# A fused transformer-and-scan kernel: the scan running on between sequences, list-scheduled engine orders, and elementwise steps on other engines

## What is computed

```
q, k, v = relu(x @ W.T + b)
attn = softmax(q @ k.T * scale);  y = relu((attn @ v) @ Wo.T + bo)
scores = sqrt(softplus(x @ gate.T)); top 2 of 8 experts by scores + gate_b
h = silu(x @ w1.T) * (x @ w3.T), times the token's weight;  out += h @ w2.T
z, x, B, C, dt = x @ W_in.T;  delta = softplus(dt @ W_dt.T + 2*b_dt)
u = silu(conv4(x) + conv_b)
state = exp(delta * A) * state + delta * u * B     # over 512 tokens, 512 channels x 16 states
y = (sum over states of state * C + u * D) * silu(z);  out = y @ W_out.T
h = relu(x @ W1.T)**2;  out = (h * rsqrt(mean(h**2))) @ W2.T
```

## Time and profile before

| | |
|---|---|
| median of three runs | 2094.04 us |
| profiled execution | 2099.33 us, of which the span is 2097.5 |
| TensorE busy | 1651.5 us (79%) |
| VectorE busy | 1770.0 us (84%) |
| ScalarE busy | 1035.9 us (49%) |
| GpSimd busy | 913.8 us (44%) |
| DMA | 157.95 MB, 75 GB/s over the span |
| granted TensorE clock, mean | 0.90 of full speed |

### The profile page before, as it was taken

The page is one execution under the profiler, slowest core; times in us unless marked ns, Lnnn a source line. Parts: engine busy times, 40 slices in busy tenths (PEclk is TensorE's granted clock), DMA queues, the critical chain, the costliest instruction groups (busy, mean ns, idle before and its releaser), DMA issues. The chain is left out here.

```text
span 2097.5 us, 22567 instructions
## 1 busy us (share of the span) xinstructions
PE 1651.5 (79%) x5875; PEld 725.3 (35%) x5948; DVE 1770.0 (84%) x3142; ACT 1035.9 (49%) x1745; POOL 913.8 (44%) x676
## 2 busy tenths in 40 slices
PE   3375577778996889868997799878997899779856
PEld 1122123232452335322452335332452335234324
DVE  6577899989879998979989998999989987987830
ACT  3247444825555454735556355734547344734312
POOL 0101534454437434554346434464346544665510
PEclk9977699979997999979997899979997899999978
DMA  4100222222222222222231222222222223223300
GB/s 108 46 0 21 72 79 89 92 69 77 75 92 65 85 71 86 85 67 78 74 101 65 81 76 76 96 75 72 76 96 71 76 85 106 86 99 113 110 10 11
DMA packets 94601, 157.95 MB, mean 75 GB/s; under 512 B 10940, under 2 KB 23660, under 8 KB 94468
## 3 DMA queue, kind: packets, MB, share of 16 engines
q1 hardware_dynamic: 94468, 156.43, 22.9%
HBM read 143.83 MB, written 12.58 MB: 75 GB/s over the span
## 5 line engine op out<-in xcount | busy, mean ns | idle before, releaser
L1226 POOL TENSOR_TENSOR prod<-state,c_all 128x512 f32<-128x512 f32 x512 | 669.6, 1312 | 706.8 <-DVE state L1203 644.0
L1203 DVE TENSOR_TENSOR_SCAN state<-decay,ps_b 128x512 f32<-128x512 f32 x512 | 619.7, 1210 | 9.7 <-issue 0.4
L750 PE MATMUL ps_y<-prod,idf 128*128 128x512 f32 x1024 | 610.6, 689 | 4.8 <-DVE u L1216 3.6
L1210 DVE TENSOR_TENSOR ps_b<-du,ps_b 128x512 f32<-128x512 f32 x512 | 347.7, 679 | 87.3 <-PE ps_b L743 86.8
L919 ACT ACTIVATE decay<-delta,a_neg 128x512 f32<-128x512 f32 x512 | 359.3, 719 | 32.3 <-DVE state L1203 29.3
L743 PE MATMUL ps_b<-b_rows,sel_b 48*128 48x512 bf16 x512 | 209.9, 411 | 155.0 <-DVE state L1203 152.7
L750 PEld LDWEIGHTS ps_y<-prod,idf 128*128 128x128 f32 x1024 | 183.8, 207 | 136.3 <-issue 109.9
L743 PEld LDWEIGHTS ps_b<-b_rows,sel_b 48*128 48x128 bf16 x512 | 47.8, 94 | 467.3 <-DVE state L1203 332.5
L619 PE MATMUL ps_x<-xT,w 128*128 128x512 bf16 (+1 forms) x391 | 132.0, 422 | 80.1 <-DVE arena_l L1095 65.6
L826 ACT ACTIVATE arena_l<-ps_x 128x512 f32<-128x512 f32 (+1 forms) x104 | 61.8, 594 | 190.8 <-PE ps_x L619 189.7
L535 PE MATMUL ps_x<-hT,win 128*128 128x512 bf16 (+1 forms) x455 | 135.6, 441 | 21.4 <-DVE arena_b L1171 16.6
(11 more groups left out here) (230 smaller groups left out, 2422.2 us busy)
## 6 DMA issues: line engine op xcount, KB each, us to landing
c_all<-c_rows SPq DMA_DIRECT2D x512, 256.0 KB
c_rows<-arena_l SPq DMA_DIRECT2D x32, 256.0 KB
out<-arena_b SPq DMA_DIRECT2D x8, 512.0 KB
x_in<-in_base SPq DMA_DIRECT2D x8, 256.0 KB
c_all<-in_winT SPq DMA_DIRECT2D x1, 1280.0 KB, 7.5
arena_b<-in_w_fc SPq DMA_DIRECT2D x1, 1024.0 KB, 5.7
arena_b<-in_w_proj SPq DMA_DIRECT2D x1, 1024.0 KB, 5.0
w<-in_w1T SPq DMA_DIRECT2D x1, 792.0 KB, 5.9
```

The source lines that it names most:

```text
L750: nc.tensor.matmul(ps_y[:], idf[:], prod[:, n % NP, :], start=(n % NST == 0), stop=(n % NST == NST - 1)).then_inc(reduced, 1)
L1203: nc.vector.tensor_tensor_scan(state[:, n % NS, :], decay[:, n % NDA, :], ps_b[:, n % NDB, :], 0.0, ALU.mult, ALU.add).then_inc(scanned, 1)
L1210: nc.vector.tensor_tensor(ps_b[:, j % NDB, :], du[:, slot(s, ct), :], ps_b[:, j % NDB, :], ALU.mult).then_inc(driven, 1)
L1226: nc.gpsimd.tensor_tensor(prod[:, n % NP, :], state[:, n % NS, :], c_all[:, n % NC, :], ALU.mult).then_inc(multiplied, 1)
```

## The change

Four things, cut from the diff:

1. Steps move. To ScalarE: rounding and eps of the bf16 norms, shift, probabilities, both ReLUs, and d_round, split into d_one (+1) and d_less (-1). To GpSimd: d_fix, d_sum and gated_y. The Exp of softmax gets scale -1, since the shift now computes max - x.
2. The gate's temporaries (g_q, g_c, g_s, g_rk, cw, cwr, g_eq and a copy of the biased scores, gate_twin) move from SBUF to bank XE of PSUM.
3. The scan's steps j go from 0 to 63 in each iteration; `tile_at` turns an index past 63 into a tile of the next sequence and one below 0 into a tile of the one before. So B's product of the next tile 0, the decay of tile 0 and the loads of C are issued at the end of an iteration, and the last scan, products, sums and the taking of y of a sequence at the begin of the next. A short piece before the first iteration and `Y_LAG` steps after the last fill and drain it.
4. `weave` replaces `in_slots` in an iteration. It lays the scan's entries and the chains' rounds on five engines with a table of durations (`BUSY`, in 10 ns), a handover of 0.12 us, a lock between VectorE and GpSimd for all steps but those in `APART`, and weights (`URGENT`); whichever can start first goes next on its engine, and among those that can start within 10 ns the one with the largest weighted rest. Each engine issues its steps in the order so found. Rounds of a chain still follow one another.

```diff
+def tile_at(s, n):
+    return (s, n) if 0 <= n < PER else (s.moved(1), n - PER) if n >= PER else (s.moved(-1), n + PER)
...
-    r = [[("V", (site, "stats"))], [("V", (site, "aggr"))], [("V", (site, "round"))], [("V", (site, "eps16"))],
+    r = [[("V", (site, "stats"))], [("V", (site, "aggr"))], [("A", (site, "round"))], [("A", (site, "eps16"))],
...
-                  (b + 6, "V", ("shift", i)), (b + 7, "A", ("exp", i)), (b + 8, "V", ("sum", i)),
-                  (b + 9, "V", ("recip", i)), (b + 10, "V", ("probs", i)),
+                  (b + 6, "A", ("shift", i)), (b + 7, "A", ("exp", i)), (b + 8, "V", ("sum", i)),
+                  (b + 9, "V", ("recip", i)), (b + 10, "A", ("probs", i)),
...
-        steps += [(k, "P", ("d", i)), (k + 1, "A", ("d_abs", i)), (k + 2, "A", ("d_exp", i)), (k + 3, "A", ("d_log", i)),
-                  (k + 5, "V", ("d_sum", i)), (k + 3, "V", ("d_round", i)), (k + 4, "V", ("d_fix", i)),
-                  (k + 6, "G", ("delta", i)), (k + 7, "G", ("du", i))]
+        steps += [(k, "P", ("d", i)), (k + 1, "A", ("d_abs", i)), (k + 2, "A", ("d_exp", i)), (k + 3, "A", ("d_one", i)),
+                  (k + 4, "A", ("d_less", i)), (k + 5, "A", ("d_log", i)), (k + 5, "G", ("d_fix", i)), (k + 6, "G", ("d_sum", i)),
+                  (k + 7, "G", ("delta", i)), (k + 8, "G", ("du", i))]
...
+def weave(chains, steps):
+    scan = {e: [(j, part) for j in steps for part in range(3) if scan_entries(e, j, part)] for e in "PAVGS"}
...
+            if offers:
+                first = min(o[0] for o in offers)
+                mine = min((o for o in offers if o[0] <= first + 1), key=lambda o: o[1])
+                if best is None or mine[0] < best[0][0]:
+                    best = (mine, e)
...
+        g_q, g_c, g_s, g_tw, g_rk, cw, cwr = (
+            ps_x[:, XE, n * NT * NEXP:(n + 1) * NT * NEXP].rearrange("p (t e) -> p t e", t=NT) for n in range(1, 8))
...
+            elif name == "shift":
+                eng.wait_ge(early["V"], ea(s, "V", ("max", i)))
+                for j in range(2):
+                    ins = act(ee[:, i % 2, j, :], ee[:, i % 2, j, :], ACT.Identity, bias=mx[:, i, j:j + 1], scale=-1.0)
...
-        def scan_dve(eng, s, j, part):
-            n = j - 1
-            if part == 0 and 0 <= n < PER:
+        def scan_dve(eng, at, j, part):
+            s, n = tile_at(at, j - 1)
+            if part == 0 and exists(s):
...
-        STEPS = range(-1, PER + 4)
+        STEPS = range(PER)
...
-            for k, (j, part, _) in enumerate(SLOTS):
-                fns["scan"](eng, s, j, part)
-                for slots in chains:
-                    run_steps(e, eng, fns, slots[k])
+            order, _ = weave(chains, STEPS)
+            for item in order[e]:
+                if item[0] == "scan":
+                    fns["scan"](eng, s, item[1], item[2])
+                else:
+                    run_steps(e, eng, fns, [item])
```

More of the change, by code:

```diff
@@ L210, in gate_rounds @@
         if i > 0:
[L211 removed]
+            r[-3].append(("G", ("gated_y", i - 1)))
     return r
@@ new lines, with name_of, busy @@
+SCAN_BUSY = {"decay": 62, "spread": 33, "drive": 60, "scan": 114, "product": 125, "sum": 87, "taken": 66, "load": 6}
+HANDOVER = 12
+APART = ("stats", "stats0", "aggr", "max", "gate_rank", "silu", "weighted", "gated", "u", "z_silu", "b_hi", "b_rest", "ms",
+         "inverse", "recip", "x4_zero")
+def name_of(step):
+    return step if isinstance(step, str) else step[1] if isinstance(step[1], str) else step[0]
+def busy(e, kind, step):
+    n = name_of(step)
+    if kind == "early" and n == "shift":
+        return 60 if e == "V" else 110
+    return BUSY.get(e, {}).get(n, 6 if e == "S" else 9)
@@ new lines, with __init__, head, take @@
+URGENT = {"late": (0.13, 0.01, 0.05, 0.01, 0.04, 0.27, 0, 0.01),
+          "early": (833.34, 11.04, 0.19, 0.09, 0.48, 11.26, 148.28, 713.24),
+          "back": (3.67, 0.96, 331.82, 0, 0.01, 0.52, 0.1, 0.02),
+          "scan": (0.78, 1.63, 7.13, 1.79, 0.8, 0.09, 0.52, 1.2)}
+class Chain:
+    def __init__(self, rounds, urgent):
+        self.rounds, self.at, self.ready = rounds, 0, 0
+        self.left = [sum(1 for _ in rnd) for rnd in rounds]
+        self.begun = [{e: 0 for e in "PAVGS"} for _ in rounds]
+        self.steps = [{e: [st for st in rnd if st[2] == e] for e in "PAVGS"} for rnd in rounds]
+        length = [max(sum(busy(e, st[0], st[3]) for st in by[e]) for e in "PAVGS") + HANDOVER for by in self.steps]
+        self.rest = [urgent[k * 8 // len(length)] * sum(length[k:]) for k in range(len(length))] + [0]
+        self.end = 0
+    def head(self, e):
+        if self.at >= len(self.rounds):
+            return None
+        k = self.begun[self.at][e]
+        return self.steps[self.at][e][k] if k < len(self.steps[self.at][e]) else None
+    def take(self, e, until):
+        self.begun[self.at][e] += 1
+        self.left[self.at] -= 1
+        self.end = max(self.end, until)
+        while self.at < len(self.rounds) and self.left[self.at] == 0:
+            self.at += 1
+            self.ready = self.end + HANDOVER
@@ L1295, in back_sync, with scan_sync @@
             eng.dma_start(seq_rows(out, s), x3).then_inc(out_stored, PER)
[L1297 removed]
+        def scan_sync(eng, at, j, part):
             if part > 0:
                 return
[L1300 removed]
+            for ahead in range(1, NC) if j == -1 else [NC - 1]:
+                s, n = tile_at(at, j + ahead)
+                if not exists(s):
+                    continue
+                last = n - NC
+                if n < NC and s.par == 0:
+                    last = max(k for k in range(PER) if c_slot(s.moved(-1), k) == n) - PER
                 stored = counted(eng, s.count(PER, PER)) if n == 0 else None
[L1302 removed]
+                used = counted(eng, s.count(PER, last + 1))
                 if n == 0:
@@ L1453, in program @@
             together(e, eng, fns, tagged("late", Seq(0), LATE), tagged("early", Seq(1), EARLY), tagged("quant", None, QUANT))
+            for part in range(3):
+                fns["scan"](eng, Seq(0), -1, part)
             iteration(e, eng, fns, Seq(0), first=True)
@@ L1459, in program @@
                 iteration(e, eng, fns, Seq(n))
+            for j in range(PER, PER + Y_LAG):
+                for part in range(3):
+                    fns["scan"](eng, Seq(NBATCH - 1), j, part)
             alone(e, eng, fns, tagged("back", Seq(NBATCH - 1), BACK))
```

306 lines of the change are left out of this document (202 added, 104 removed), and 2 rows, old and new, of the table b.

## The result

The kernel after takes 2010.35 us (median of four runs, 2006.57 to 2023.95), against 2094.48 for the kernel before on the same chip: a ratio of 0.961, 95% interval 0.9563 to 0.9658. It is faster, as forecast, but by 84 us where 239 were forecast, and it lies outside the range of 1780 to 1950. The profiled execution is the slowest of the four, 2023.95 us; 14 us of what its rows show are not in the median.

What follows compares the result with a forecast made beforehand. The prediction took VectorE to bound the kernel, TensorE close behind. Full sequences -189, sequence 0 -31, sequence 6 -23, sequence 7 -6, start +9, tail +1 sum to -239 us: 2099.3 to 1860 profiled, 1855 median, range 1780 to 1950.

Steps and rivals of the forecast that it cites:

- VectorE's need (186): Full sequence: VectorE's busy time falls from 217 to 186 us through moved steps and the gate's temporaries in PSUM.
- table loads: ScalarE's activation table loads: between none and 4 more a sequence, 0 to 5 us.
- Before the first scan: Stretch ahead of sequence 0's first scan: nothing fills the gaps, so +9 us, bounds 0 and +20.
- The orders ... I take 14 us: Full sequence: under the new orders VectorE idles 14 us, between bounds of 1 and 20, so it takes 200 us.
- TensorE's own need: Full sequence: TensorE's 202 us busy includes slow-clock stretches; at full clock it needs 186 us, level with VectorE.
- Both receiving engines have over 50 us a sequence free: ScalarE and GpSimd, full sequence: the argument against moved steps binding there, as each has over 50 us free.
- rival D: Moved steps bind on ScalarE and GpSimd: 36 us a sequence stand for 28.6, no change, 2094 us; chance 0.02.
- The change of sequence: Border between sequences, VectorE busy 6.3 of 16 us: the running scan closes it, gaining some 5 us.
- No stretch of 16 us with a single scan: Sign that the forecast holds: in full sequences no 16 us would pass with only one scan.
- Rival C: TensorE is the new bound or a static order goes out of step: 215 us a sequence, 1945 us; chance 0.25.
- A static order goes out of step: The other half of Rival C, beside TensorE as the new bound, sharing its 1945 us and chance 0.25.

Runs made afterwards that it cites:

- The first experiment: The kernel after with the old slots and a scan ending inside its sequence (moves without the new order): 2135.04 us, ratio 1.0189 to the kernel before.

## Why the prediction was wrong

**VectorE's need (186): right.** 189.98 measured. The gate's temporaries in PSUM did leave the wait: the L1016 form of the earlier trace rows, 1035 ns, is 421 now (L1206), near its shortest of 394 before; while L1197, which still reads both operands from SBUF, takes 979 (165 to 1253). That is the exclusive lock which the Trainium skill describes in SBUF — State Buffer (who interferes with whom), and the rows agree. ScalarE 149.93 (146 forecast; a shift is 714 ns, not 622), GpSimd 124.87 (132; its steps take 1.27 us, not 1.47), table loads 77 in all, 67 before (and 79 in the new order with the old steps, so they rise with the order). Before the first scan 244.5 (240.5). Together these terms are off by under 30 us over the kernel, VectorE's 4 us in each full sequence among them.

**"The orders ... I take 14 us": this step failed.** The idle time is 31.8 us, 17.8 more; with the 4 of VectorE this is the 22 us by which each full sequence misses. The 14 was taken between 1 and 20, both read where VectorE had its old work. It held that an engine with less work would not idle longer than before. The first experiment shows the opposite: of 27.8 us taken off VectorE all became idle time in the old slots, and more. In the new order 20.6 us came off (210.59 to 189.98), and the five full sequences got 5.2 us shorter on average (227.2 to 222.0), while the first scan came 11 us later (233.2 to 244.5). The steps of the other engines, and the order that they stand in, had become the limit: 33 us came back with two of GpSimd's steps made small and 26 with other weights.

**"TensorE's own need" (186 us at full clock): not reached.** Its busy time is 196.87 at a clock of 0.94, over the 195 that the prediction itself named as a sign of being wrong. It cost little, as the bf16 products show: 34 us less on TensorE are 5.7 us of the sequence. In sequence 6 the same term was 173 and measured 183.09. In sequence 0 VectorE came out at 175.23 (180 forecast) and idled 25 us where 10 were taken: the step on idle time again.

**"Both receiving engines have over 50 us a sequence free": the wrong measure.** This set rival D at 0.02, and D is near to what the moves alone did, at an even higher price (+40 us, where D said no change). The row that spoke against it was on the page: in the last slice of the earlier trace rows GpSimd is busy 24.25 of 35.9 us, 68%, against 49% over the sequence. Eight more steps of 1.27 us, 10.2, all softplus steps that fall late in the sequence, bring that to 34.4 of 35.9. The trace after shows 28.28 of 30.70. The small d_fix and d_sum put 33 us on these two steps, 5.2 of them in each full sequence. But with the steps back on VectorE the end of the sequence was no shorter, though GpSimd had 8 us less to do there. A full queue on GpSimd alone doesn't account for both. The chain through the two steps would: it takes 2.59 us on GpSimd (1320 + 1269 ns) and still 2.00 on VectorE (1136 + 863). No run separates the chain from the queue.

**The change of sequence.** The gap stays, moved by a tile (12.0 us against 9.6), and 8 us of stall in it come with the added wait, which no part of the sum held. Shortened, it gives 8 us in all. "No stretch of 16 us with a single scan" did not come true either: in sequence 4 there is one scan, at 1241.7, between those that start at 1236.0 and 1254.7. Inside it TensorE is full and VectorE is not:

```profile
1237.00:1253.00 16.00, 15.89 (x107) 10.97 (x107) 11.22 (x32) 6.56 (x11) 7.92 (x3) 1.00 0.21 71
```

**Rival C (1945).** TensorE's clock was 0.94 and its busy time 196.87, near C's 202, and the sum came out on C's side and past it. But TensorE as the bound is refuted: 34 us less work gave 5.7 in sequence 4. "A static order goes out of step" is nearer. Flat weights cost 175 us, other weights and the shorter wait give 34. That shows that the order sets the time; that it goes out of step with its own plan is not shown, for no run sets the plan's times beside the trace's.

**What the miss is made of.** Of the 155 us, other weights with the shorter wait account for 34, the bf16 sums for 25 on top, GpSimd's two steps for 24 on top: 83, to 1927. The last 72 are still there with all of them relieved. By that kernel's trace 56 lie in sequences 1 to 5 (211.3 us each on average, not 200), 2 ahead of the first scan, 2 in sequence 6 and 11 in sequence 7 and the tail, while sequence 0 is 6 under its forecast; the other 6 come from setting medians beside traces: the forecast's median lies 5 us under its own trace, this kernel's time 1 us over its. What the remaining idle time waits for was not taken apart: its cause stays open. No run tried an order that is built with the measured lengths.

## What to carry to other kernels

Work moved to an engine that is free on average costs what it costs in the stretch where it lands: read that engine's busy share there, add the moved steps, count the chain through them at its new length, and only then call it free. When the bounding engine's work falls by an eighth, expect the idle time to grow, as the steps on the other engines come next; one run with the work taken off and the order kept shows it. A busy share near 100% on another engine doesn't prove that it bounds either: make its instructions shorter and look. For each step that is moved, list the buffers it reads and who overwrites them: the wait moves too, and may now end with something much later on the new engine.

## What the runs showed of the hardware

The moved steps and their neighbours on GpSimd ran at 1.27 to 1.32 us for 128x512. delta fell from 1473 ns to 1268; with d_fix, d_sum and gated_y back on VectorE and ScalarE's steps left there it is 1472 again. So the longer delta goes with these steps on VectorE, not with those that went to ScalarE. TensorE's sums and its B products, by line, in the kernel before and in the same with bf16 products:

```profile
L750 PE MATMUL ps_y<-prod,idf 128*128 128x512 f32 x1024 | 610.6, 689 | 4.8 <-DVE u L1216 3.6 <-POOL prod L1226 1.1
...
L743 PE MATMUL ps_b<-b_rows,sel_b 48*128 48x512 bf16 x512 | 209.9, 411 | 155.0 <-DVE state L1203 152.7 <-DVE er L990 0.6
```

```profile
L750 PE MATMUL ps_y<-prod,idb 128*128 128x512 bf16 x453 | 211.0, 480 | 12.2 <-DVE u L1216 6.4 <-POOL prod L1226 4.4 <-issue 1.3
...
L743 PE MATMUL ps_b<-b_rows,sel_b 48*128 48x512 bf16 x512 | 236.0, 462 | 299.5 <-DVE state L1203 288.5 <-issue 6.4 <-DVE er L990 1.3
```

An fp32 sum has two records and a bf16 sum one, so 512 are to be expected and 59 are missing. All 512 would be busy some 238 us, an estimate from the 211.0 of the 453; that is some 370 us less than before. Only 246 show in TensorE's busy time (1651.5 to 1405.9). The B products, which the edit doesn't touch, take 462 ns instead of 411. The granted clock was lower at the same time: in the first quarter of sequence 4 it was 0.91 before and 0.67 with the bf16 products. In the last eighth of after's sequence 4 it went from 0.75 with TensorE busy 17.55 of 30.7 us to 0.50 with 12.54 busy, that is from between the two levels to 1.2 GHz throughout. Less work on TensorE was in part paid back by slower work on the rest.
